# A graph transformer layer on one core: products of a constant block between TensorE's stages

## The reference

```python
xn = _layernorm(x)
x = x + gnn(xn, src, dst, ...) + mix(xn[None], ...)[0]
x = x + ffn(_layernorm(x)[None], Wr, W1, W2)[0]
```

## Time and profile before

| what | value |
|---|---|
| median of three runs | 1608.07 |
| the profiled execution, device time | 1608.05 |
| its span, first to last instruction | 1606.4 |
| mean granted clock of TensorE | 0.970 |
| TensorE matmuls busy | 92% of the span, 7927 instructions |
| DVE busy | 51% |
| ACT busy | 32% |
| POOL busy | 11% |
| share of TensorE in the chain that ended last | 77% |

### The profile page before, as it was taken

One profiled execution on the slowest core, in us unless ns is written; L12 is line 12 of the kernel. 1 busy time (PEld: TensorE's weight loads), 2 busy tenths in 40 slices (PEclk: granted clock), 3 DMA queues, 4 the chain that ended last, 5 costly groups with the idle time before them and its releaser, 6 DMA issues.

```text
span 1606.4 us, 20299 instructions
## 1 busy us (share of the span) xinstructions
PE 1481.5 (92%) x7927; PEld 1374.0 (86%) x7927; DVE 819.8 (51%) x1502; ACT 510.2 (32%) x596; POOL 182.5 (11%) x183
## 2 busy tenths in 40 slices
PE   3899999999999999999999999999989829999996
PEld 2889898989898989889999999999877728998885
DVE  6546565656556565662356533355466634344330
ACT  4233333333333333323212123332211114444441
POOL 0011010101010101000000000000000252432321
PEclk8899999999999999999999999999999958999998
DMA  9622222223131313838544113331454467888764
GB/s 290 221 35 48 55 48 54 48 55 50 53 51 52 51 51 51 291 115 203 136 109 113 49 46 101 104 93 33 119 160 148 129 176 199 196 211 228 181 152 80
DMA packets 75158, 184.10 MB, mean 115 GB/s; under 512 B 10937, under 2 KB 41648, under 8 KB 73345
## 3 DMA queue, kind: packets, MB, share of 16 engines
q1 hardware_dynamic: 54296, 135.59, 28.0%
q0 software_dynamic: 20768, 47.22, 16.4%
HBM read 124.66 MB, written 68.01 MB: 120 GB/s over the span
## 4 chain that ended last, share of the span: by engine, by line
PE 77%; DVE 8%; ACT 6%; DMA 5%; issue 2%; POOL 1%; SPq 0%; POOLq 0%; ACTq 0%; DVEq 0%
PE slot L1566 30%; PE slot L1635 11%; PE slot L1810 6%; PE slot L1737 6%; PE slot L1778 6%; PE slot L1722 3%; PE kvb L1810 3%; DMA adj_d<-stage 2%; PE slot L1713 2%; PE kvb L1690 2%; PE slot L1793 1%; DMA mix_d<-mixn 1%; PE lsb L1676 1%; PE slot L1676 1%; DVE kk_l L1286 1%
## 5 line engine op out<-in xcount | busy, mean ns | idle before, releaser
L1566 PE MATMUL slot<-big_hi,slab_h 128*128 128x418 f32 x960 | 247.6, 366 | 17.0 <-DVE big_lo L1044 5.5
L1566 PE MATMUL slot<-big_lo,slab_h 128*128 128x418 f32 x960 | 238.9, 357 | 0.0
L1566 PE MATMUL slot<-big_hi,slab_l 128*128 128x418 f32 x960 | 236.7, 355 | 0.0
L1566 PEld LDWEIGHTS slot<-big_hi,slab_h 128*128 128x128 f32 x960 | 176.5, 192 | 25.4 <-DVE big_lo L1044 6.1
L1566 PEld LDWEIGHTS slot<-big_lo,slab_h 128*128 128x128 f32 x960 | 183.7, 191 | 2.7
L1566 PEld LDWEIGHTS slot<-big_hi,slab_l 128*128 128x128 f32 x960 | 182.9, 191 | 2.9
L732 POOL DMA_DIRECT2D adj_d<-stage x80 | 67.6, 845 | 552.2 <-ACT stage L812 359.7
L1635 PE MATMUL slot<-adj,xs_h 125*128 125x418 f32 x480 | 118.2, 354 | 0.8 <-DVE ztmp L1044 0.5
L1635 PE MATMUL slot<-adj,xs_l 125*128 125x418 f32 x480 | 117.4, 353 | 0.0
L1048 DVE TENSOR_SCALAR oh_src<-lane,src_lo 125x125 bf16<-125x125 f16 x320 | 82.3, 257 | 20.5 <-PE lsb L1498 15.2
L1635 PEld LDWEIGHTS slot<-adj,xs_h 125*128 125x128 f32 x480 | 90.4, 189 | 2.2 <-DVE ztmp L1044 0.7
(11 more groups left out here) (289 smaller groups left out, 2748.1 us busy)
## 6 DMA issues: line engine op xcount, KB each, us to landing
slab_raw<-slabs_dram SPq DMA_DIRECT2D x48, 512.0 KB, 3.7
ws_raw<-w_dram SPq DMA_DIRECT2D x36, 512.0 KB
adj_d<-stage POOLq DMA_DIRECT2D x81, 117.2 KB, 3.1
w_raw<-w_dram SPq DMA_DIRECT2D x9, 1024.0 KB
adj_d<-eye_dram POOLq DMA_DIRECT2D x1, 6250.0 KB, 25.4
raw<-adj_d SPq DMA_DIRECT2D x3, 1828.8 KB
dx<-x_dram SPq DMA_DIRECT2D x10, 448.0 KB
xn_d<-dx SPq DMA_DIRECT2D x10, 448.0 KB
```

Of the source, the lines that this page charges most:

```text
L1566: mm = ten.matmul(ps[:, 512 * q:512 * q + CW], w[a][:, kt, :], big[b][:, kt, CW * q:CW * q + CW], start=(kt == 0 and c == 0), stop=(kt == ...
```

## The change

A helper, `keep_running(n)`, issues n products of ones_r by ones_r (128 stationary columns, 128 moving columns, fp32r) into slot0, columns 1024 to 1151. Nothing waits for these products, nothing reads what they write, and they carry no semaphore. It is called at five places in TensorE's order:

- 24 products behind the transposes of the last tile of the start, in front of V 0 and its waits;
- 95 products in front of FT 9 and its wait;
- 300 products behind the waits for the number of rounds and SL, in front of the register read and the loop;
- 30 products each in XE 0, 1 and XE 0, 2, in front of the wait for the gather (behind the wait for the PSUM half, where there is one);
- 24 products in GA 0, 0, behind the wait for WP 0 and in front of the wait for the split of XE 0, 3.

```diff
+            def keep_running(n):
+
+                for _ in range(n):
+                    ten.matmul(slot[0][:, 1024:1152], ones_r[:, :], ones_r[:, :], start=True, stop=True)
+
...
                 if k in AMID.values():
                     continue
+                if k == ("V", 0):
+                    keep_running(24)
+                if k == ("FT", NT - 1):
+                    keep_running(95)
...
             ten.wait_ge(rounds_ready, 1)
             ten.wait_ge(dve_done, DVED[("SL", LAST)])
+            keep_running(300)
             rounds = ten.value_load(rounds_n[0:1, 0:1], min_val=1, max_val=ROUNDS)
...
                     if kind == "XE":
                         e, i = k[1:]
+                        if e == 0 and i in (1, 2):
+                            keep_running(30)
                         ten.wait_ge(gathered[e % 2][i], r * (16 * EXP // 2) + 16 * (e // 2 + 1))
...
                         dved(("WP", m))
                         if kind == "GA" and k[2] == 0:
+                            if k[1] == 0:
+                                keep_running(24)
                             dved(("XE", k[1], NRT - 1))
```

## The result

The changed kernel took 1660.84 us (median of five runs, 1660.21 to 1666.03) against 1608.07 before (median of five as well, 1605.29 to 1611.51): a ratio of 1.0338, with a 95% interval of 1.0316 to 1.036. It is slower by 53, where 15.7 was forecast and 1628 was the upper end of the range. The profiled execution took 1660.84, with a span of 1659.2.

What follows compares the result with a forecast made beforehand. The prediction took TensorE to bound the kernel, its chain gapless from the first expert's gate products on. First expert 18.1 later, less 2.4 at V 0, gave +15.7 on 1608.05: 1623.8 us, range 1600 to 1628.

Steps and rivals of the forecast that it cites:

- The price at full clock: All five fillings: one new product costs 0.111 us at 2.4 GHz, taken from the router's fp32r row.
- the first rival: All fillings: each product costs 0.0575, so the fillings fit their holes and the kernel ends at 1600.7; chance 0.18.
- the price between: All fillings: a product costs about 0.08, ending at 1608.4, no change; chance 0.07.
- The half-clock price: All fillings: one new product costs 0.21 us at 1.2 GHz, from the router's 250-column steps and eight transposes.
- FT 9, +3.2: In front of FT 9: 95 products take 10.6 and push it by 4.4, full clock returns 1.2; routing 3.2 later.
- V 0, 2.4: In front of V 0: 24 products fill the hole, V 0 starts at full clock and saves 2.4 (0 to 2.6).
- 300 products: In front of the expert loop: 33.4 at full clock plus 1.9 for one slow start, ending at 1338.6.
- the next step: XE 0 and GA 0, 0: new products and transposes at full clock; first gate products end at 1355.8, 18.1 later.
- The third rival: All fillings: unread products of this kind don't hold the clock up, so the kernel ends near 1405 there, 1675 overall; chance 0.04.
- The one-sided part of the forecast: FT 9 and the loop: fillings outlast their holes, 95 taking 10.6 against 6.08 and 300 taking 33.4 against 17.3.

Runs made afterwards that it cites:

- e13_ft300: Kernel of e6_front with 300 narrow products in place of the 95 in front of FT 9, none in front of the expert; 1629.18 us, ratio 1.0126.
- e5_first: The changed kernel with only the 24 products in front of V 0, all other calls of keep_running removed; 1605.19 us, ratio 0.9988 to the kernel before.
- e6_front: The changed kernel with only the 24 in front of V 0 and 95 in front of FT 9; 1607.32 us, ratio 1.0001 to the kernel before.
- e1_data: The changed kernel with the 300 products multiplying real values (big_hi by big_hi, same shape and type) instead of constant ones; 1665.62 us, ratio 1.0362.
- e3_prime: The changed kernel with 16 products of 512 columns put in front of the 300 narrow ones; 1657.75 us, ratio 1.0318 to the kernel before.
- e4_f16: The changed kernel with the 300 as f16 products of 125 by 125 ones by 125 columns; 1614.73 us, ratio 1.0046 to the kernel before.
- e8_best: The changed kernel with hole-sized fillings: 50 before FT 9, 64 of 512 columns for the 300, wide ones in XE and GA; 1600.92 us, ratio 0.9964.
- e10_prime90: The changed kernel with 16 products of 512 columns and 90 narrow ones in place of the 300; 1618.36 us, ratio 1.007 to the kernel before.
- e11_no300: The changed kernel without the 300 products in front of the loop, all else kept; 1615.83 us, ratio 1.0053 to the kernel before.

## Why the prediction was wrong

**The price at full clock** was right: 0.111 a product, and neither 0.0575 nor 0.08. With that the first rival and the price between are out. The 95 in front of FT 9 took 10.66 on the chain (10.6 in the text), the 300 of e13_ft300 33.55.

**The half-clock price** was right too: 0.21 taken, 0.214 measured. Of its two sources only the router's row gives it: the eight transposes of 105 columns, read as 0.21 each from their 1.66, take 1.42 on the chain after, 0.18 each.

**FT 9, +3.2**: right in the profile to a tenth, counted from when TensorE arrives there. The last routing operation of DVE, after:

```profile
1296.67 0.14 DVE L1420 CAST rounds_n<-nw 1x1 int32<-1x1 f32 x1
```

It stood at 1299.95 before. TensorE arrived at the 95 products 6.5 earlier than before (1273.90 against about 1280.4), and 6.5 less 3.2 is the 3.3 by which this is earlier. By the medians of e5_first and e6_front the step costs 2.1, with the doubt said above.

**V 0, 2.4**: the mechanism is right where the clock is up, as in the profile of after. TensorE then reached the next wait, for kT_l, 2.3 earlier once the 0.9 is taken off by which this execution's start was ahead. Behind it came 1.5 more, because a slow stretch between 85 and 90 fell away, and some 1.8 by the end of the middle that I have not traced. As a saving to be counted on it was too large: V 0 began at full clock in eight of thirteen profiles, and the runs of the 24 alone show 2.

**The step that failed** is in "300 products": "It was idle for almost 3 us again, so I count one slow start: in 4 us at 0.21 go 19 products". That taking-up time was read from rows in which wide products raised the clock (418 columns behind V 0, 250 in the router), and laid on products that stream 128 columns in the same step. They never raised it. The block took 64.26 instead of 35.3 (33.4 and 1.9): 29.0 of the miss. The same error stands in the next step: the 60 and 24 products, the transposes and the first gate products took 30.0 (1361.13 to 1391.12) instead of 16.9 at full clock: 13.1. Less 4.1 by which the front was ahead of the forecast (6.5 less 2.4) and 0.3 for the register read, which the chain does not show, that is the 37.7 between 1353.4 (1355.8 less 2.4) and 1391.12.

**The third rival** was near in time (1675) and had 0.04. Its time came near by luck: it had the 95 at half clock as well, which they were not. It said that unread narrow products do not hold the clock. They do; they only did not bring it back. Its argument against, "transposes alone raised the clock before 45.02", was sound for transposes, and I should have asked for the same evidence for the narrow fp32r product: the router's 126-column products ran at 1.00, but the clock had been raised by the 250-column ones in front of them. Rows that show a product at full clock say nothing of what that product does from half clock.

The one-sided part of the forecast, that the fillings are longer than their holes, holds also without the clock: e13_ft300 shows 300 at full clock to be 33.6 long, and the hole is 17.3.

## What to carry to other kernels

A filler that is to keep TensorE's clock must be able to raise it as well, or the first hole before it turns it into a load at half speed: here 256 or 512 columns of fp32r to a product and 125 of f16 did, 128 columns of fp32r did not. In these traces the rise took 3.3 to 6.2 us of such work. Size a filler by the hole at full clock and leave it a little short, since every product over it is paid in full, and at double price when the clock is low. Read separately which rows show a clock being held and which show it rising, and by what products.

## What the runs showed of the hardware that was not expected

- 128 stationary by 128 moving columns in fp32r held 2.4 GHz for 33.55 us (e13_ft300) and stayed at 1.2 GHz for 64.26 us (the change, e1_data), both times without a break. Twice the columns at the same half-clock step left 1.2 GHz after 3.3 us. The Trainium skill, "TensorE: Matmul & The Clock Gate", in "Why this matters for your kernels", asks only that TensorE be kept busy continuously to reach the full clock. The 64 us here, busy without a break, show that this is not enough.
- Transposes can raise the clock, and do not always: behind sixteen of 105 columns it rose in two of seven profiles, and in the kernel before it came up while only transposes of 125 columns had run since 38.7. These are the stretches (before, as in the earlier trace rows):

```profile
43.00:44.00 1.00, 1.00 (x5) 1.00 (x6) 0.23 (x1) 1.00 (x3) 0.00 (x0) 0.50 1.06 366
44.00:45.00 1.00, 0.82 (x5) 0.53 (x3) 1.00 (x2) 0.02 (x1) 0.00 (x0) 0.71 0.75 262
```

  The Trainium skill, "TensorE: Matmul & The Clock Gate", says in "Part 4: PE-mode transpose" that the full clock does not engage for them; these rows differ.
- Under POOL's gathers a dense stream of short products got holes of 0.1 to 1.0 for which no counter was awaited (e3_prime at a DMA share of 1.02 to 1.08, e4_f16 from 0.81 on). In front of the gathers it had none, at shares up to 1.74 (e13_ft300). The cause is open.
- The clock fell in or just behind holes of 1.03 to 1.31 (in front of V 0 in e3_prime, e4_f16 and e8_best; in front of XE 0, 0 in e10_prime90), and stayed up across one of 1.03 in front of V 0 in others (the change, e11_no300) and one of 1.23 behind wide products (e8_best).
- Whether the clock is up after the start's transposes changes from run to run: the profiles show all three courses with the same program up to there, so a saving there is an average over them.
